# First pass, tiles 3 to 31: the result is turned by VectorE's block transposes and a round trip through DRAM in place of TensorE's identity products, and the landed data is taken ahead of layer 0

## The reference

```python
x = x + s4(cond(x, cond_512, first weights))      # first pass
x = x + ffn(cond2(x, cond_512, second weights))   # second pass
```

## Time and profile before

| what | value |
|---|---|
| median of 3 runs | 1317.92 us (1317.89 to 1319.16) |
| profiled execution | 1320.42 us, its span 1318.6 us |
| PE busy | 97% of the span, DVE 79%, POOL 70%, ACT 64% |
| mean granted clock of PE | 0.991 of full speed |
| chain that ended last | PE 87%, DVE 5%, POOL 4%, ACT 2% |

### The profile page before, as it was taken

One profiled execution on the slowest core, in us unless ns is written; L12 is line 12 of the kernel. 1 busy time (PEld: TensorE's weight loads), 2 busy tenths in 40 slices (PEclk: granted clock), 3 DMA queues, 4 the chain that ended last, 5 costly groups with the idle time before them and its releaser, 6 DMA issues.

```text
span 1318.6 us, 23280 instructions
## 1 busy us (share of the span) xinstructions
PE 1276.2 (97%) x8214; PEld 1220.5 (93%) x8214; DVE 1043.9 (79%) x2311; ACT 842.3 (64%) x1772; POOL 916.6 (70%) x730
## 2 busy tenths in 40 slices
PE   3789999999999999999999999999999999999999
PEld 3578899999899999999999999999999999999998
DVE  7777878777877777877878888788887878788872
ACT  4577777778777877776556555565656565565640
POOL 6458888666666777666768766676776767676752
PEclk9789999999999999999999999999999999999999
DMA  3234455445544554455443342433425252433433
GB/s 131 78 92 138 124 142 150 133 122 146 134 135 135 137 136 138 131 151 147 85 130 105 101 134 79 126 109 111 124 83 152 79 149 86 131 104 114 121 85 90
DMA packets 86278, 158.23 MB, mean 120 GB/s; under 512 B 26634, under 2 KB 48403, under 8 KB 86035
## 3 DMA queue, kind: packets, MB, share of 16 engines
q1 hardware_dynamic: 84898, 154.79, 41.8%
q10 hardware_dynamic: 1264, 1.96, 0.5%
HBM read 93.79 MB, written 33.56 MB: 97 GB/s over the span
## 4 chain that ended last, share of the span: by engine, by line
PE 87%; DVE 5%; POOL 4%; ACT 2%; issue 1%; DMA 1%; SPq 0%; POOLq 0%; DVEq 0%; ACTq 0%
PE psum L1905 28%; PE psum L1907 28%; PE psum L1906 27%; PE psum L2036 2%; POOL xs_l L964 1%; DMA w3T<-in_w_dram 1%; POOL vs_l L959 1%; POOL as_l L993 1%; PE psum L289 1%; DVE vm_l L1635 0%; POOL vbuf L943 0%; POOL vbuf L939 0%; DVE turned L1685 0%; DVE a_l L1662 0%; PE psum L2203 0%
## 5 line engine op out<-in xcount | busy, mean ns | idle before, releaser
L1905 PE MATMUL psum<-wt_h,u_h 128*128 128x386 f32 (+1 forms) x760 | 261.2, 344 | 0.0
L1907 PE MATMUL psum<-wt_h,u_l 128*128 128x386 f32 (+1 forms) x760 | 258.3, 340 | 0.0
L1906 PE MATMUL psum<-wt_l,u_h 128*128 128x386 f32 (+1 forms) x760 | 258.0, 340 | 0.0
L939 POOL TENSOR_TENSOR vbuf<-vbuf 128x512 f32<-128x512 f32 x64 | 97.7, 1526 | 170.4 <-ACT vbuf L1260 170.4
L1685 DVE STREAM_TRANSPOSE turned<-vbuf 32x256 f32<-32x256 f32 x480 | 208.9, 435 | 7.9 <-ACT vbuf L1246 0.7
L953 POOL TENSOR_TENSOR vm_f<-vm_f 128x512 f32<-128x512 f32 x64 | 82.8, 1293 | 120.8 <-DVE vm_l L1635 120.4
L1253 ACT ACTIVATE vbuf<-psum,tabs 128x512 f32<-128x512 f32 x128 | 105.2, 822 | 93.2 <-PE psum L1907 89.6
L1905 PE MATMUL psum<-a_h,vm_h 128*128 128x256 f32 x512 | 148.4, 290 | 3.2 <-ACT vbuf L1253 3.0
L1906 PE MATMUL psum<-a_l,vm_h 128*128 128x256 f32 x512 | 146.0, 285 | 0.0
L1907 PE MATMUL psum<-a_h,vm_l 128*128 128x256 f32 x512 | 145.8, 285 | 0.0
L1905 PEld LDWEIGHTS psum<-wt_h,u_h 128*128 128x128 f32 x760 | 143.7, 189 | 0.5
(11 more groups left out here) (336 smaller groups left out, 4187.5 us busy)
## 6 DMA issues: line engine op xcount, KB each, us to landing
vm_f<-vv SPq DMA_DIRECT2D x256, 112.0 KB, 4.3
xin<-in_x_ph_dram SPq DMA_DIRECT2D x32, 512.0 KB, 5.0
xr<-in_x_row_dram SPq DMA_DIRECT2D x32, 512.0 KB, 3.9
x1d<-xr SPq DMA_DIRECT2D x64, 256.0 KB, 3.3
xin<-x1d SPq DMA_DIRECT2D x32, 512.0 KB, 4.0
xr<-x1d SPq DMA_DIRECT2D x64, 256.0 KB, 5.2
xo<-in_b_base_dram SPq DMA_DIRECT2D x32, 512.0 KB, 5.6
out_dram<-xo SPq DMA_DIRECT2D x31, 512.0 KB, 2.8
```

The lines of the kernel that those rows point to most:

```text
L939: G.tensor_tensor(v3[:, :, 1:H:2], v3[:, :, 1:H:2], by_odd, ALU.subtract).then_inc(v3_odd, 1)
L1905: nc.tensor.matmul(to, stat_h, mov_h, start=first_ and n == 0, stop=False, skip_group_check=True)
L1906: nc.tensor.matmul(to, stat_h, mov_l, start=False, stop=False, skip_group_check=True)
L1907: ins = nc.tensor.matmul(to, stat_l, mov_h, start=False, stop=end, skip_group_check=True)
```

## The change

For tiles g = 3 to 31 (`spun(g)`) PE's `turn` goes. Instead:

1. DVE's `spin(g)`, after layer0(g+1) and ahead of composed2(g+1), writes the row ends and turns the result in two transposes of [128 partitions x 512] that swap positions only inside blocks of 32x32, into `xo`.
2. SP stores `xo` to DRAM (`spin`, 512 KB), waits for that, waits for the end of s4(g-1), and loads it back by four DMAs of 32 partitions each, with the blocks in their places. This is at the head of SP's body g+1.
3. `landed(g)` in body g+1: ACT, after third(g+1) is taken out and ahead of layer0(g+2), copies `u_h` in two pieces and then `s_h`; DVE, ahead of layer0(g+2), adds the sums, makes `u_l` in two pieces, and makes `s_l` too (before, POOL's).
4. PE makes step1(i+2) ahead of s4(i-1), and s4 waits for `u_lo` itself; layer0(i+1) does not wait for `u_lo` any more.
5. DVE's `u_l` and even_and_odd at the head of the body go, ACT's `u_h` and `s_h` there go, POOL's `s_l` goes, ACT's row_ends go. ACT's evacuation of pair(i,0) waits for the transposes of tile i-1.

```diff
+SPUN = 3
+        sh.spin = nc.dram_tensor("spin", [P, L], F32, kind="Internal").ap()
...
+    u_spun = [view(t, 0, (512, 2), (32, 2), (64, 8), (1, 32)) for t in (u_h, u_l)]
+    with ExitStack() as landing:
+        s_in = sb("s_in", [P, 3 * P], F32, landing)
     s_l = sb("s_l", [P, 3, P], FR)
+    s_spun = [view(t, 0, (32, 2), (64, 6), (1, 32)) for t in (s_h, s_l)]
+    s_runs = view(s_in, 0, (32, 2), (64, 6), (1, 32))
+    u_runs = view(xo, 0, (512, 2), (256, 2), (32, 8), (1, 32))
...
+            def spin(g):
+                sp.wait_ge(tr_done, at(g))
+                sp.dma_start(sh.spin, xo[:, :]).then_inc(spin_out, 16)
+                sp.wait_ge(spin_out, 16 * (g - SPUN + 1))
+                sp.wait_ge(s4_done, at(g - 1))
+                for t in range(4):
+                    src = bass.AP(tensor=sh.spin.tensor, offset=sh.spin.offset + 2 * P * t, ap=[[L, 32], [32 * L, 4], [1, 2 * P]])
+                    sp.dma_start(xo[32 * t:32 * t + 32, :].rearrange("p (f n) -> p f n", f=4), src).then_inc(u_land, 16)
             def body(i):
+                if spun(i - 1):
+                    spin(i - 1)
...
+            def landed(g):
+                act.wait_ge(u_land, 64 * (g - SPUN + 1))
+                for q in range(2):
+                    ins = A(u_spun[0][:, q], u_runs[:, q], ACT.Copy)
+                ins.then_inc(u_hi, 1)
...
                 if here(i):
                     pair_evacuated(i, 1)
                     third_evacuated(i)
+                if spun(i - 1):
+                    landed(i - 1)
+                    act.wait_ge(sum_ready, at(i - 1))
+                    A(s_spun[0], s_runs, ACT.Copy).then_inc(s_hi, 1)
...
+            def landed(g):
+                ve.wait_ge(u_land, 64 * (g - SPUN + 1))
+                V.tensor_tensor(s_runs, u_runs[:, 0, :, 0:6], u_runs[:, 1, :, 0:6], ALU.add).then_inc(sum_ready, 1)
+                ve.wait_ge(sum_ready, at(g))
+                ve.wait_ge(u_hi, at(g))
+                for q in range(2):
+                    ins = V.tensor_tensor(u_spun[1][:, q], u_runs[:, q], u_spun[0][:, q].bitcast(F32), ALU.subtract)
+                ins.then_inc(u_lo, 1)
+                ve.wait_ge(s_hi, at(g))
+                V.tensor_tensor(s_spun[1], s_runs, s_spun[0].bitcast(F32), ALU.subtract).then_inc(s_lo, 1)
+            def spin(g):
+                c, t = place(g)
+                ve.wait_ge(v3_val, at(g))
+                if group(g) is not None:
+                    ve.wait_ge(sh.vfix_ready, group(g) + 1)
+                V.tensor_copy(v3[:, :, 0:H:H - 1], sh.vfix[:, c, batches(t), :]).then_inc(v3_fix, 1)
+                ve.wait_ge(v3_fix, at(g))
+                ve.wait_ge(s_lo, at(g - 1))
+                for b in range(2):
+                    ins = V.transpose(view(xo, 32 * b, (256, 4), (64, 4), (1, 32)),
+                                      v3[:, b, :].rearrange("p (n t x) -> p t n x", t=4, x=32))
+                ins.then_inc(tr_done, 1)
...
                 row_ends(i)
                 if second(i - 1):
                     inserted(i)
+                if spun(i - 1):
+                    landed(i - 1)
                 if here(i + 1):
                     layer0(i + 1)
+                if spun(i):
+                    spin(i)
...
+                if spun(g):
+                    pe.wait_ge(u_lo, at(g))
...
+                if spun(i - 1) and here(i + 2):
+                    pe.wait_ge(blur, at(i + 1))
+                    step1(i + 2)
                 if first(i - 1):
...
-                if here(i) and not by_blocks(i):
+                if here(i) and not by_blocks(i) and not spun(i):
```

More of the change, by code:

```diff
@@ L576, in program @@
     in_scaled = sem("in_scaled")
+    spin_out, u_land = sem("spin_out"), sem("u_land")
     ms_sum, ms_hi, ms_lo = sem("ms_sum"), sem("ms_hi"), sem("ms_lo")
@@ L695, in nth, with spun @@
         return n * (g - HALVED) + i + 1
+    def spun(g):
+        return here(g) and SPUN <= g < TILES
     def turned_f(g):
@@ L998, in body @@
                     pair_sums_low(i)
-                if first(i - 1):
+                if first(i - 1) and not spun(i - 1):
                     sum_low(i - 1)
@@ L1313, in body @@
                     turned(i - 1)
+                elif spun(i - 1):
+                    if here(i):
+                        act.wait_ge(tr_done, at(i - 1))
+                        pair_evacuated(i, 0)
                 else:
@@ L1838, in body @@
             def body(i):
-                if here(i - 1):
+                if here(i - 1) and not spun(i - 1):
                     turned(i - 1)
-                if first(i - 1):
+                if first(i - 1) and not spun(i - 1):
                     even_and_odd(i - 1)
@@ L2040, in rows, with s4_rows @@
                 return (u_h[:, k, :, :].rearrange("p b c -> p (b c)"), u_l[:, k, :, :].rearrange("p b c -> p (b c)"))
+            def s4_rows(g, k):
+                if spun(g):
+                    return [view(t, 512 * (k % 2) + P * (k // 2), (1, P)) for t in (u_h, u_l)]
+                return rows(k)
             def s4(g, i):
@@ L2047, in s4 @@
                     pe.wait_ge(toep_lo, 1)
-                product(ps_tail, [(*rows(7 - r), sh.tail_h[:, r, :, :].rearrange("p q n -> p (q n)"),
+                if spun(g):
+                    pe.wait_ge(u_lo, at(g))
+                product(ps_tail, [(*s4_rows(g, 7 - r), sh.tail_h[:, r, :, :].rearrange("p q n -> p (q n)"),
                                    sh.tail_l[:, r, :, :].rearrange("p q n -> p (q n)")) for r in range(2)], True, True)\
@@ L2057, in s4 @@
                     for j in range(3):
-                        st = (s_h[:, j, :], s_l[:, j, :]) if stat is None else rows(2 * j + stat)
+                        st = (s_h[:, j, :], s_l[:, j, :]) if stat is None else s4_rows(g, 2 * j + stat)
                         n = H - P * j
@@ L2162, in body @@
                 if here(i + 1):
-                    if here(i - 1) and not by_blocks(i - 1):
+                    if here(i - 1) and not by_blocks(i - 1) and not spun(i - 1):
                         pe.wait_ge(u_lo, at(i - 1))
@@ L2188, in body @@
                     ffn(1)
-                if here(i + 2):
+                if here(i + 2) and not spun(i - 1):
                     if here(i + 1):
```

## The result

The changed kernel takes 1430.1 us (median of three runs, 1428.4 to 1431.3) against 1318.4 us before (four runs, 1317.9 to 1319.2): ratio 1.0846, 95% interval 1.0824 to 1.0867. It is slower, as forecast, but 49 us above the predicted 1381 and 5 us under the upper end of the range. A fourth execution of the changed kernel took 2103.9 us at a mean granted clock of 0.64 and is left out, as a slow one; no other kernel here had such an execution. The profiled execution took 1431.25 us, its span 1429.4.

The account below looks back on a forecast made before the run. The prediction took a ring of waits through PE, ACT and DVE as the bound: 3.5 us come in, 1.3 were slack, so bodies go from 15.47 to 17.65 us, 61 us over 28, plus 2: 1381 us (range 1350 to 1435).

Parts of the forecast that it names:

- The prediction's ring: Waits through PE, ACT and DVE, gone round once per tile; forecast to lengthen a body from 15.47 to 17.65 us.
- DVE, added in landed(i-1): DVE's sums, `u_l` and `s_l` for landed data: nothing in the ring; without cover by ACT up to 1.7 us.
- rival A: DVE's transposes run at the copy's rate: 0.55 us less in a body, 1366 us; chance 0.12.
- the section on the reorder array: Rule on DVE's transposes, one element per cycle per lane: two would cost about 1.2 us; the sum took 1.75.
- rival B: The DRAM round trip's landing sets the pace if over 10.3 us; for 12 us, 1429 us; chance 0.16.
- rival C: PE's clock falls after idle time, doubling at most 4.06 us on PE per body: 1495 us; chance 0.05.
- rival D: Faster: PE sets the pace with 14.6 us, landed data taken in existing waits: 1293 us; chance 0.09.
- my 25.2: PE's predicted saving in us from losing 29 turns, each 0.79 us and 0.08 for a later start.
- PE with its 15.47 sets the pace by little: Before the change, PE's 15.47 us body was put only slightly above the closed-up ring's 14.2 us.
- 1.3 us of slack: Waits in the ring before the change: 0.61 at `c_l`, 0.36 on ACT, 0.15 and 0.2 estimated.
- PE's busy share: Sign: falls from 97% to about 92%, with idle time before step2 and before pair or third.
- SP costs nothing: Five more DMA issues per body on SP add nothing; if SP were late, `vm_l` has some 2 us.

Follow-up runs that it names:

- pool_quiet: The changed kernel with POOL's `combined` cut to a few columns in tiles 3 to 31 (result left wrong): 1368.7 us, ratio 1.037.
- landed_behind: The changed kernel with the landed data taken behind layer 0 on ACT and DVE, instead of ahead of it: 1492.6 us, ratio 1.1313.
- pool_waits: The changed kernel with one wait more: POOL's `combined` also waits for DVE's `s_l` of the landed tile: 1441.8 us, ratio 1.093.
- flat_runs: The changed kernel with `u_l`, `s_l`, ACT's copies and the sums over contiguous rows instead of runs of 32: 1429.0 us, ratio 1.0828.
- store_twice: The changed kernel with the store to DRAM made twice in a row, the loads waiting for both: 1431.5 us, ratio 1.0853.
- spin_late: The changed kernel with DVE's `spin(i)` at the end of the body, behind `composed1`, instead of ahead of `composed2`: 1502.5 us, ratio 1.1402.
- no_turn: The kernel before with seven of the eight identity products of tiles 3 to 31 left out, nothing in their place: 1313.9 us, ratio 0.9956.
- order_only: The kernel before with only PE's `step1(i+2)` moved ahead of `s4(i-1)`, in tiles 4 to 31: 1318.7 us, ratio 0.9998.
- behind_filled: landed_behind with 28 more PE products per tile, ahead of s4's wait for `u_lo`, their output overwritten: 1438.7 us, ratio 1.0905.
- s_low_on_pool: The changed kernel with `s_l` of tiles 3 to 31 made by POOL behind `combined` instead of by DVE: 1424.4 us, ratio 1.0795.

## Why the prediction was right in direction and 49 us low

The prediction's ring, in the body above. Times are from the start of ACT's evacuation of `third` (308.99 in the prediction's sum, 348.33 here).

| point of the ring | predicted | measured | this step's error |
|---|---|---|---|
| ACT's second `a_h` ends | 5.06 | 4.71 | -0.35 |
| DVE's `a_f` ends | 6.54 | 8.59 | +2.40 |
| transposes end | 8.44 | 10.01 | -0.48 |
| `c_l` ends | 13.19 | 14.68 | -0.08 |
| step2 starts | 13.27 | 14.74 | -0.02 |
| next evacuation starts | 17.65 | 19.25 | +0.13 |

- **The mechanism is right, one term is not.** Over 28 bodies 1.60 us make 45 of the 48 us by which the profiled time (1431.25) passed its prediction (1383.4); most of the rest is body 32, which with body 3 took 4.6 us more than before, where +2 was forecast.
- **The step that failed** is "*DVE, added in landed(i-1)* ... Nothing in the ring; without that cover up to 1.7 us". It had the durations of `u_l` and `s_l` from operations that ran alone (0.6 each and 0.5), and 4.33 us measured are far beyond the cover: they end 1.8 us behind ACT's second `a_h`, with both `a_l` still to do. A DVE operation on two SBUF operands and POOL's operations shut each other out: pool_quiet takes POOL's away and gets 16.94 us per body (the prediction's own terms with the two measured savings, 0.35 and 0.48, would give 17.65 - 0.83 = 16.82); landed_behind and pool_waits keep them apart with all work left in and get 712 and 688 ns, 565 and 550 ns; flat_runs excludes the pattern. Both sides pay: POOL's L967 and L969 take 1.37 and 1.84 us when crossed (run beside the other engine's), 1.04 and 1.52 alone. Not every DVE operation is hit: `a_l`, which reads one of its large operands from PSUM, takes 0.75 us at 313.07 beside POOL's L943, and 0.74 to 0.76 in all 70 cases before, 66 of them beside a POOL operation.
- The Trainium skill has this rule: "SBUF — State Buffer", section "🔬 SBUF: two separate sides", says that the port pair shared by DVE and GpSimd is an exclusive lock held for a whole instruction, and that a DVE operation with two SBUF inputs takes part in it against a GpSimd operation that reads SBUF. The runs agree. The prediction weighed POOL only as someone who waits, not as someone who is in the way. The trace of before had the sign, in the range of one line (ns, min/median/max). Its longest is the second of the two here, beside a POOL operation of the start; 96 of the 128 have no POOL operation beside them and take 677 to 693.

```profile
L1635 DVE TENSOR_TENSOR vm_l<-vm_f,vm_h x128: 677/685/1961, 45.1 to 1276.9; 128x512 fp32r<-128x512 f32 x128
...
101.98 2.56 DVE L1635 TENSOR_TENSOR vm_l<-vm_f,vm_h 128x512 fp32r<-128x512 f32 x2
...
101.97 2.02 POOL L868 TENSOR_TENSOR wsq<-wT 64x768 f32<-64x768 f32 x1
```

- **Transposes** (rival A): two take 1.22 us by their spacing, so A's value was the right one, not the 1.75 that I took from the row of 32 partitions. A's rate is confirmed, A's time is not, since the other term outweighs it. The prediction's estimate by the section on the reorder array (the Trainium skill, "Vector Engine (DVE) Microarchitecture Reference", section 3.8, one element per cycle per lane) was about 1.2 for two; this shape agrees with it, at 1.22.
- **The landing** (rival B): the last load is issued 4.0 us after the transposes' end (358.34 to 362.3) and loads land in 2.9 us (2.5 to 3.4), so the data is there by 364.8 to 365.7, some 7 us after the transposes where I took 9.3. DVE's sums come at 366.7 and ACT's `u_h`, which is in the ring, at 368.5. Hidden, by 2.8 to 3.7 us; store_twice used it up without loss. In spin_late ACT and DVE do wait for it. That the rival's number, 1429, is the time measured is chance.
- **The clock** (rival C): 0.96 over bodies 4 to 32 after the change, against 1.00. Plain bodies at 0.91 last 19.4 to 19.7 us instead of 19.25, little. landed_behind shows that C was a real danger, at an idle time of 4.07 us; the changed kernel's plain bodies have up to 1.47.
- **Faster** (rival D): no_turn puts the gain of nearly the whole turn (seven of its eight products) at 5.4 us of my 25.2, even with nothing in its place. "PE with its 15.47 sets the pace by little" was true to a greater degree than my 1.3 us of slack said.
- PE's busy share fell to 90% (92 forecast), with idle time at `c_l`, and hardly any before `pair` (6.7 us in all for DVE's `xr`); that before s4 (43.1 us for `u_l`, 15.7 for `s_l`) I had not named. SP costs nothing, as said (ACT's `vm_h` waits 3.4 us in all for DMAs, 6.0 before), nor does step1's place (order_only).

**What stays open.** That the ring is longer by spin's operations on DVE and the landed copies on ACT is read from the timelines; no run takes one of them out alone. No version with all its work beat the kernel before. A version with s4 two tiles behind, in which the landed data would be taken in waits that stand late in the body, was not tried, since its buffers and waits would have to be made anew; if it had the same ring of ACT and DVE, no_turn would put its gain at some 5 us at most (an estimate). Nor was pool_waits with `vm_l` ahead of the transposes, which could fill its 2.12 us. Of behind_filled, 0.8 us per body above the expectation isn't accounted for.

## What to carry to other kernels

A duration read from an operation that ran alone holds only where it will again run alone: before work is put on DVE, look at what POOL does at that moment, and at the maximum of such operations, not their mean. An engine that is busy for 97% may still be worth almost nothing; leave its work out once and see what ring closes. When a gap opens on PE, ask what clock the work behind it will get.

## What the runs showed that I had not expected

- Making POOL wait shortened five operations and gained nothing for the ring: DVE's row-end copy starts at 8.4 us with turns (pool_waits) and at 8.5 crossed, although the work on both engines ends at 8.4 and at 6.5.
- After 4.07 us without a product, PE worked at a granted clock of 0.57 for the next 4 us; 812 products with no use made the kernel 54 us faster (behind_filled).
- Shorter idle times can stand ahead of a lower clock too: 1.39 and 1.27 us close together, then 0.63 over 4 us (s_low_on_pool); 2.17 us, then 0.50 (pool_waits), and the same 2.17 us without a fall one body earlier.
- A round trip of 512 KB through DRAM: store 2.6 us to landing (2.6 to 2.9), four loads 2.9 us (2.5 to 3.4), where the nearest rows of before had 2.8 and up to 7.4.
